# A metaformer layer on one core: router logits taken chunk by chunk, fillers tied to router steps, and one dispatch piece moved to GpSimd and ScalarE

## What is computed

```python
x = x + attention(layernorm(x))          # 12 heads of 32, decomposed relative positions
t = x.reshape(8, 128, 384)               # 8 groups of 128 tokens
tn = layernorm(t)
logits = einsum('gsd,de->gse', tn, w_router)          # 8 experts
gate, idx = top_k(softmax(logits), 2)
prio = place of each token among those that chose the same expert   # cumsum of one-hot masks
dispatch = one_hot(prio, C=40)                        # [g, s, e, c]
expert_in = einsum('gsec,gsd->egcd', dispatch, tn)
h = relu(expert_in @ wi[e]);  expert_out = h @ wo[e]  # F = 1536
t = t + einsum('gsec,egcd->gsd', dispatch * gate, expert_out)
```

## Time and profile before

| | us |
|---|---|
| median of 3 runs (603.87 to 604.47) | 604.02 |
| profiled execution, its own time | 604.96 |
| its span, first to last instruction | 603.2 |
| TensorE busy in the span | 589.5 (98%) |
| VectorE, ScalarE, GpSimd busy | 383.1, 295.2, 196.2 |
| mean granted TensorE clock | 0.993 |

### The profile page before, as it was taken

One profiled execution on the slowest core, in us unless ns is written; L12 is line 12 of the kernel. 1 busy time (PEld: TensorE's weight loads), 2 busy tenths in 40 slices (PEclk: granted clock), 3 DMA queues, 4 the chain that ended last, 5 costly groups with the idle time before them and its releaser, 6 DMA issues.

```text
span 603.2 us, 11469 instructions
## 1 busy us (share of the span) xinstructions
PE 589.5 (98%) x4459; PEld 510.8 (85%) x4459; DVE 383.1 (64%) x643; ACT 295.2 (49%) x411; POOL 196.2 (33%) x115
## 2 busy tenths in 40 slices
PE   8999999999999999999989999999999999999996
PEld 7887976766677666668978999999999999999994
DVE  6546787776776766723888965545566545367525
ACT  4555245544555545563556434453546444455523
POOL 2300068888898888898000000000000000000000
PEclk9999999999999999999899999999999999999999
DMA  8046064444333344103322444443443444443302
GB/s 272 12 87 133 1 132 88 89 89 83 65 66 69 67 87 87 41 2 106 126 71 79 158 158 156 140 145 132 140 153 96 151 148 158 158 156 93 104 1 104
DMA packets 38614, 63.39 MB, mean 105 GB/s; under 512 B 3912, under 2 KB 34478, under 8 KB 38446
## 3 DMA queue, kind: packets, MB, share of 16 engines
q1 hardware_dynamic: 38574, 62.83, 36.9%
HBM read 44.16 MB, written 1.57 MB: 76 GB/s over the span
## 4 chain that ended last, share of the span: by engine, by line
PE 93%; DVE 4%; ACT 2%; issue 1%; POOL 0%; DVEq 0%; POOLq 0%
PE ps L815 21%; PE ps L831 21%; PE ps L588 14%; PE ps L597 9%; PE ps L493 8%; PE ps L575 7%; PE ps L525 2%; DVE rhalf L1181 2%; PE ps L458 1%; PE ps L786 1%; PE ps L536 1%; PE ps L475 1%; PE ps L842 1%; PE ps L761 1%; PE ps L621 1%
## 5 line engine op out<-in xcount | busy, mean ns | idle before, releaser
L1181 DVE TENSOR_REDUCE rhalf<-ps 128x1 f32<-128x512 f32 x192 | 131.6, 690 | 33.6 <-PE ps L575 32.4
L415 POOL TENSOR_TENSOR acc<-acc,prob 128x1024 f32<-128x1024 f32 x58 | 139.6, 2408 | 8.8 <-ACT prob L972 4.3
L972 ACT ACTIVATE prob<-ps 128x1024 f32<-128x1024 f32 x96 | 98.0, 1027 | 82.5 <-PE ps L588 81.9
L588 PE MATMUL ps<-qst,kst 128*128 128x512 f32 x384 | 115.5, 397 | 0.9 <-ACT prob L972 0.9
L443 POOL CAST dpc<-dpt 120x1024 fp32r<-120x1024 f32 (+1 forms) x3 | 3.1, 1040 | 274.3 <-PE ps L851 216.6
L815 PE MATMUL ps<-xeh,wih 128*128 128x320 f32 x288 | 89.6, 311 | 1.0 <-ACT xeh L1036 1.0
L831 PE MATMUL ps<-hh,woh 128*128 128x320 f32 x288 | 89.2, 310 | 0.0
L831 PE MATMUL ps<-hh,wol 128*128 128x320 f32 x288 | 89.0, 309 | 0.0
L815 PE MATMUL ps<-xeh,wil 128*128 128x320 f32 x288 | 89.0, 309 | 0.0
L831 PE MATMUL ps<-hl,woh 128*128 128x320 f32 x288 | 89.0, 309 | 0.0
L815 PE MATMUL ps<-xel,wih 128*128 128x320 f32 x288 | 89.0, 309 | 0.0
(11 more groups left out here) (162 smaller groups left out, 883.5 us busy)
## 6 DMA issues: line engine op xcount, KB each, us to landing
raw_i<-in_L_ffn_wi SPq DMA_DIRECT2D x32, 576.0 KB, 5.2
raw_o<-in_L_ffn_wo SPq DMA_DIRECT2D x32, 576.0 KB, 4.1
xs<-in_x SPq DMA_DIRECT2D x8, 384.0 KB, 4.4
qst<-qh SPq DMA_DIRECT2D x12, 256.0 KB, 3.1
qst<-relh SPq DMA_DIRECT2D x12, 256.0 KB, 3.9
qst<-relw SPq DMA_DIRECT2D x12, 256.0 KB, 4.4
kst<-kp SPq DMA_DIRECT2D x12, 256.0 KB, 5.1
qst<-ql SPq DMA_DIRECT2D x12, 128.0 KB, 3.1
```

Of the source, the lines that this page charges most:

```text
L415: nc.gpsimd.tensor_tensor(acc[:, :], acc[:, :], prob[:, slot_of(j, t), :], ALU.add).then_inc(sum_add, 1)
L588: last = mm(bank(2 * (t % 2) + half), kst[b][:, part, t * P:(t + 1) * P], qst[b][:, part, half * BANK:(half + 1) * BANK], start=part == 0, ...
L972: run(prob[:, slot_of(j, t), :], ps[:, 2 * (t % 2) * BANK:2 * (t % 2 + 1) * BANK], ACT.Exp).then_inc(exp_done, 1)
L1181: ve.tensor_reduce(rhalf[:, p // 2, p % 2:p % 2 + 1], bank(4 + p % 2), AX_X, ALU.max).then_inc(max_red, 1)
```

## The change

- The logits wait for the copy of each chunk, not for all three, and go chunk by chunk over the four tiles. Only the very first matmul into bank 7 starts an accumulation.
- In the first half a single `keep_on(1, 6)` follows each chunk; `keep_on(2, 6)` behind the half is gone.
- `keep_on(15, 6)` behind the logits becomes 6, then 3 behind `rt_step` 13, then 1 behind `rt_step` 22.
- VectorE compares three dispatch pieces, not four. For the last, GpSimd subtracts `pos` from the slot numbers into a new tile `apart` and squares it, and ScalarE writes `relu(1 - apart)` into `dsp` behind its sixth `xeh` copy. Steps 9 to 11 of the dispatch wait for that.
- `pos` has a semaphore of its own; the `dg` product waits for all four pieces.

```diff
@@ tiles, helper
+    apart = new("apart", [P, XT * E, C])
+        def dispatch_pair(g):
+            ge = [P, XT * E, C]
+            return (dsp[:, g:g + XT, :, :].rearrange("p g e c -> p (g e) c"), slot1[:, :].unsqueeze(1).broadcast_to(ge),
+                    pos[:, g:g + XT, :].rearrange("p g e -> p (g e)").unsqueeze(2).broadcast_to(ge))
@@ gpsimd, behind the bias additions
+            pool.wait_ge(pos_ready, 1)
+            to, numbers, places = dispatch_pair(NT - XT)
+            nc.gpsimd.tensor_tensor(apart[:, :, :], numbers, places, ALU.subtract).then_inc(apart_pool, 1)
+            pool.wait_ge(apart_pool, 1)
+            nc.gpsimd.tensor_tensor(apart[:, :, :], apart[:, :, :], apart[:, :, :], ALU.mult).then_inc(apart_pool, 1)
@@ tensor
                 keep_on(5, 6)
-                pe.wait_ge(turn_act, 4 * DC + (3, 5)[half])
-                pe.wait_ge(turn_dve, 4 * DC + half)
-                for g in range(half * HALF, (half + 1) * HALF):
-                    for c in range(DC):
+                for c in range(DC):
+                    pe.wait_ge(turn_act, 4 * DC + ((1, 2, 3), (4, 4, 5))[half][c])
+                    if half == 1 and c == 1:
+                        pe.wait_ge(turn_dve, 4 * DC + 1)
+                    for g in range(half * HALF, (half + 1) * HALF):
                         last = mm(bank(7)[:, g * E:(g + 1) * E], tnT[:, c, g * P:(g + 1) * P], wrt[:, c, :],
-                                  start=c == 0, stop=c == DC - 1)
-                if half == 0:
-                    keep_on(2, 6)
+                                  start=c + g == 0, stop=c == DC - 1, skip_group_check=True)
+                    if half == 0:
+                        keep_on(1, 6)
             last.then_inc(logits_mm, 1)
-            keep_on(15, 6)
+            keep_on(6, 6)
+            pe.wait_ge(rt_step, 13)
+            keep_on(3, 6)
+            pe.wait_ge(rt_step, 22)
+            keep_on(1, 6)
             pe.wait_ge(masks_ready, 2)
...
-                pe.wait_ge(dsp_ready, n // DC + 1)
+                if n < 3 * DC:
+                    pe.wait_ge(dsp_ready, n // DC + 1)
+                else:
+                    pe.wait_ge(dsp_act, 1)
@@ scalar
                 run(*expert_input(n, 0), ACT.Copy).then_inc(xe_act, 1)
+                if n == 2 * DC - 1:
+                    act.wait_ge(apart_pool, 2)
+                    run(dispatch_pair(NT - XT)[0], apart[:, :, :], ACT.Relu, scale=-1.0, bias=ones[:, 0:1]).then_inc(dsp_act, 1)
@@ vector
-            step(ve.tensor_tensor(pos[:, :, :], cm1[:, :, :], cm2[:, :, :], ALU.add))
-            ge = [P, XT * E, C]
-            for g in range(0, NT, XT):
-                ve.tensor_tensor(dsp[:, g:g + XT, :, :].rearrange("p g e c -> p (g e) c"), slot1[:, :].unsqueeze(1).broadcast_to(ge),
-                                 over(pos[:, g:g + XT, :].rearrange("p g e -> p (g e)"), C), ALU.is_equal).then_inc(dsp_ready, 1)
+            ve.tensor_tensor(pos[:, :, :], cm1[:, :, :], cm2[:, :, :], ALU.add).then_inc(pos_ready, 1)
+            dve.wait_ge(pos_ready, 1)
+            for g in range(0, NT - XT, XT):
+                ve.tensor_tensor(*dispatch_pair(g), ALU.is_equal).then_inc(dsp_ready, 1)
...
+                        dve.wait_ge(dsp_ready, 3)
+                        dve.wait_ge(dsp_act, 1)
                         ve.tensor_tensor(dg[:, :, :, :].rearrange("p g e c -> p (g e) c"),
```

More of the change, by code:

```diff
@@ L153, in metaformer_layer @@
     woh, wol = (new(n, [P, 2, UF, D], F32R) for n in ("woh", "wol"))
+    XT = 2
     end, at[0] = at[0], at[0] - 8 * UF * D
@@ L160, in metaformer_layer @@
     idxf = new("idxf", [P, NT, 2])
+    apart = new("apart", [P, XT * E, C])
     lmax, lsum, lrec = (new(n, [P, NT]) for n in ("lmax", "lsum", "lrec"))
-    assert at[0] <= end and max(top, end) <= nc.sbuf_usable_end
+    end = max(end, at[0])
+    assert max(top, end) <= nc.sbuf_usable_end
     ctx = ExitStack()
@@ L177, in wait @@
                 eng.wait_ge(s, value)
-        XT = 2
         x_in = [sem(f"x_in{n}") for n in range(NT // XT)]
@@ L208, in metaformer_layer @@
             sem(n) for n in ("th_ready", "tl_ready", "logits_mm", "rt_step", "ex_ready", "masks_ready", "count_mm"))
-        dsp_ready, dg_ready, gsl_ready = (
-            sem(n) for n in ("dsp_ready", "dg_ready", "gsl_ready"))
+        pos_ready, dsp_ready, apart_pool, dsp_act, dg_ready, gsl_ready = (
+            sem(n) for n in ("pos_ready", "dsp_ready", "apart_pool", "dsp_act", "dg_ready", "gsl_ready"))
         dpt_mm, dpt_dve, xe_mm, xe_act, xe_dve = (
```

## The result

Over 12 runs each, the changed kernel takes 605.35 us in the median (604.58 to 607.69) and the one before 603.99 (602.84 to 607.11). Single runs far off the rest, such as 726.6 and 3259 us among the twelve of the moved piece alone, are left out of all medians and ratios. The prediction said 602.1 with a range from 601.3 to 605.4 and forecast faster. The direction was wrong.

The account below looks back on a forecast made before the run. TensorE, on the chain for 93% of the span, was taken as the bound, its waits before the expert matmuls deciding. Terms -1.39 - 0.76 + 0.18 = -1.97 us took 604.02 to 602.05, said as 602.1, range 601.3 to 605.4.

Parts of the forecast that it names:

- (g), the moved piece: Last dispatch piece on GpSimd and ScalarE: VectorE's three pieces run unbroken, GpSimd starts 2.27 us late, still before ScalarE asks.
- this rival, the one on the slower side: Dispatch: GpSimd gets in between VectorE's pieces, +1.57 us each; one handover 603.6, two 605.2; chance 0.30.
- the main case: Whole change: the clock holds and VectorE's pieces run unbroken, likeliest 602.05 us, own range 601.4 to 602.8; chance 0.40.
- (b): Second half's turns: fillers between narrow matmuls keep the clock at 2.4 GHz, turns take 1.31 us, -1.39 us.
- (g), the Relu: ScalarE's dispatch copies: the new Relu delays its seventh copy, then VectorE's copy 8 by about +0.18 us, bounds 0 and +0.7.
- (f): Dispatch: one piece of 0.757 us leaves VectorE's path between `pos` and the first `xel` copy, -0.76 us.
- (a): First half's logits: chunk waits bring nothing; six filler instructions take 0.67 us, so turns may start at 298.41, before at 298.78.
- (c): Second half's logits chunk by chunk: needed copies lie under the fillers, chunk waits cost and bring 0, logits end at 303.43.
- (d): VectorE's queue before it reads the logits: ends 0.15 us ahead of them, so the 1.39 us passes through whole.
- (e): Fillers behind the logits held by router steps: direct cost 0, and 0 taken for the clock.
- a rival of 0.10: Clock falls later, at the count matmuls: +0.65 to 1.5 us, 602.7 to 603.5; chance 0.10.

Follow-up runs that it names:

- the moved piece alone: Kernel before with only the dispatch change (three VectorE pieces, the last on GpSimd and ScalarE), logits and fillers as they were: 605.67 us, ratio 1.0029.
- memsets: Changed kernel with all four pieces on VectorE and four GpSimd memsets of `apart` beside them, unused: 602.73 us in a single run.
- late GpSimd: Changed kernel with GpSimd waiting for VectorE's third dispatch piece before its subtraction: 603.49 us, ratio 0.9980; again 602.95, ratio 0.9978.
- the logits part alone: Kernel before with only the chunk-by-chunk logits and a filler pair behind each first-half chunk: 604.03 us, ratio 0.9986; again 603.76, ratio 0.9995.
- the kernel without a moved piece: Changed kernel with VectorE's four dispatch pieces of before, so both filler changes only: 603.19 us, ratio 0.9986; again 603.84, ratio 0.9983.

## Why the prediction was wrong

**(g), the moved piece.** This step failed. It let VectorE's three pieces run unbroken, with GpSimd waiting behind them. GpSimd got in after the first piece and again after the second. The row for it stood in the text: the addition of 3.31 us that went on about when VectorE's reads ended. I gave this rival, the one on the slower side, 0.30 and put the main case on the other. So the sum held nothing for it, where 2.13 us was measured (4.42 against 2.29). The rival's price was 1.57 for each handover, from GpSimd rows of 384 and 1024 elements. Measured were 1.07 and 1.06; 640 elements took 1.26 unheld, and why VectorE loses less than that no run shows. That its total of 605.2 came close to 605.35 is in part luck: its two handovers were 1.0 too dear, and (b) gave 1.39 where both filler changes together gave about 0.9. The lock that the Trainium skill states (SBUF — State Buffer, section "SBUF: two separate sides") holds here as told, also in that a GpSimd instruction which doesn't read SBUF stays out of it (3.03 with memsets).

**(g), the Relu.** Named +0.18 with bounds 0 and 0.7. With the late GpSimd the stretch is 11.60 where 11.99 - 0.76 = 11.23 would leave no cost, so +0.37 was lost; 0.27 of it is VectorE's wait behind the Relu, for the rest no row stands. (f)'s gain of 0.76 is real, but half of it is given back here.

**(b), the clock.** Named -1.39. In the two profiles the stretch shortens by 1.57, so it looked right. But the other two traces with the old logits part read 10.96 and 11.22. Where the clock does not fall ahead of the turns, the change saves 0.14 (10.96 to 10.82), or 0.27 where it falls within the second logits (11.22 to 10.95). The term was read from a single execution and carried to the median of all. The runs of the logits part alone bound it at -1.8 to +0.5 us, the ends of its two intervals.

**(a)** came out 0.18 shorter than said: the half's logits and fillers took 3.35 us (three times 0.79 and 0.32) and not 2.86 + 0.67 = 3.53. That is the difference between 1.57 and 1.39.

**(c) and (d)** held. The chunk waits cost and brought nothing, and VectorE's queue was free 0.30 us before the logits (predicted 0.15).

**(e), the fillers.** Named 0, with +0.65 at the least as a rival of 0.10. In the profile after it was +0.66: at 1.2 GHz the later fillers and the counts are slow. Over the runs it is no loss, because the 15 fillers lose 0.16 to 0.42 themselves where the clock falls in or behind the logits (four traces). The prediction did not see that side, as before's own trace had no such fall.

Put together: the moved piece +1.74 by its stretch, which is -0.76 for the piece, +2.13 for the two handovers and +0.37 (alone it has the ratio 1.0029, the same 1.75 us), and the filler changes about -0.9 (0.9986 and 0.9983; their intervals span -1.8 to +0.2). That gives +0.8 to +0.9. Measured was +1.9 (1.1 to 2.7), or 1.4 between the medians. The gap of about 1 us is not clear of that spread. If it is real, the clock is a candidate: 4 of the changed kernel's 12 runs have a granted clock of 0.989 or less, and they are its slowest (606.6 to 607.7), while of the 94 runs of the kernel before that were taken beside the experiments 6 have one so low. It may have fallen in the dispatch steps, as the trace of the moved piece alone has it, or for longer at the count matmuls, as in the profile after. No run tells the two apart, so this stays open.

## What to carry to other kernels

Work handed from VectorE to GpSimd to run beside it is not free if both read two tensors from SBUF at that moment: let it start when VectorE turns to PSUM, and the same work no longer holds VectorE up. Before a stall by the clock is booked as a gain, look whether it comes in more than one execution. Fillers that wait for a step of another engine overran the step behind them in one trace of nine when the clock was low, and by 0.2 us; a fixed count did so in all four traces with such a fall.

## What the runs showed of the hardware

Of VectorE instructions with two SBUF inputs queued one behind the other, GpSimd got one of its own in at each boundary, in all three traces where it could. The group took 4.42 us twice, and 3.36 with one instruction; the changed kernel's 1.90 and 1.71 against 1.26 and 1.25 unheld are GpSimd's side of it. VectorE's queue did not keep the port. Four memsets of 640 elements in the same place moved nothing. And the granted clock fell at different places in executions of the same instructions: with the new logits and the held fillers it was 1.2 GHz from 303.6 to 307.0 in one trace of the kernel without a moved piece and never between 295 and 325 in the other. Runs of the kernel before range over 602.84 to 607.11.
